# A four-stage language tower on one core: when the stages' semaphores are cleared, and when the experts' scatters may follow each other

## The chip, the core and the metric

The kernel runs on one core of a Trainium2 chip. The metric is the device time of one execution in microseconds. Three runs are known of the kernel before: 2097.66, 2103.85 and 2105.65 us, median 2103.85. The program of a core is five instruction streams: TensorE (PE), VectorE (DVE), ScalarE (ACT), GpSimd (POOL) and SyncE (SP). They meet only at semaphores.

## The reference

Eight sequences of 512 tokens go through a tower of width 192, all in 32-bit floats:

```
h = embedding(x)                                       # 8 x 512 x 192
h = h + rwkv_attention(layernorm(h))
h = h + mixture_attention_ffn(layernorm(h))            # 4 nested experts and 12-head attention
h = h + state_space_block(layernorm(h))
h = h + experts(layernorm(h))

def experts(flat):                                     # 4096 rows of 192
    p, i = top_k(softmax(flat @ Wr), 2); p = p / sum(p)
    for e in 8 experts:                                # the 1280 rows that weigh most
        rows, w = the 1280 best rows of expert e and their weights
        y = (silu(flat[rows] @ w1[e]) * (flat[rows] @ w3[e])) @ w2[e]
        out[rows] += w * y                             # scatter with addition
    return out + (silu(flat @ s1) * (flat @ s3)) @ s2  # the shared expert
```

## The kernel before

The tower is written as four stages, one after the other: `embed_and_route` (embedding, first attention, routing), `moe_attention_ffn`, `state_space_block` and `experts_tower`. Each stage stands in `with kit.phase()` (L42), and inside it has one block with an instruction stream for every engine. At the end of a block all engines drain and meet at a barrier; in the trace its records carry L45. A stage makes its own semaphores through `kit.sem`, which notes them in `kit.used`: 41, 32, 50 and 47 in the four stages. Semaphores that GpSimd's own transfers raise come from `pool_dma_sem`, belong to the whole program and are never cleared. After the stage's block, `phase` opens a second block in which only SyncE has anything to do: it clears the semaphores of `kit.used` one by one (L53). This block too ends with a barrier of all engines (records at L49). Then the next stage begins. SyncE's stream in a stage begins with the loads of weights: L900 in the attention stage, L1602 in the state-space stage, L2384 to L2388 in the experts' stage. Behind them come its waits: for the split parts in `parts_to_scratch` (L906), for the convolution in the state-space stage, for the rows dealt to the experts (`scattered`, L2389) in the last.

The last stage first computes the shared expert for all 4096 rows and routes; GpSimd scatters the rows to a table `dealt` in memory, 1280 slots per expert. The expert loop then takes 40 tiles of 256 rows (`TILES`), five per expert (`CHUNKS`), two blocks of 128 rows each (`CB`). For a tile n:
- SyncE loads the rows (`load_rows`), and TensorE transposes them (`turned_rows`).
- GpSimd takes the rows' weights and numbers out of the tile (`meta`, L2465) into one of two buffers, `w_of` and `row_of`.
- TensorE makes gate and up products (`row_halves`, `whole_rows`), ScalarE the silu (L2943), VectorE the product (`times_gate`).
- TensorE multiplies by w2 (`outputs`, L2877), one tile behind: `outputs(n)` follows `whole_rows(n + 1, 2)`. It waits for VectorE's reading of the tile before (`oe_ready`), as both blocks of a tile lie in one bank of PSUM.
- VectorE weights the two blocks into a buffer `o[:, n % 2]` (`weighted`, L2685).
- GpSimd adds them to the output in memory with two indirect transfers (L2483), one per block, and then waits until both have landed (`stored`, L2488) and raises `oe_free`. So the scatters of two tiles never are in flight together.

`kit.apart` (L59) is a semaphore increment that GpSimd issues ahead of a group of indirect transfers. A wait in the code is taken by the instruction that follows it in the engine's stream.

Of the kernel before, what the change touches and what calls it, by code (L numbers as in the profile page):

```python
# [12 lines left out]
P = 128  # L13
C = 192
# [20 lines left out]
class Kit:  # L35

    def __init__(self, nc, ctx):
        self.nc, self.ctx, self.whole, self.used = nc, ctx, ctx, []

    @contextmanager
    def phase(self):  # L42

        outer, self.used = self.ctx, []
        with ExitStack() as self.ctx:  # L45
            yield self.ctx
        self.ctx = outer

        with self.nc.Block() as block:  # L49
            @block.sync  # L50
            def _(sp):
                for x in self.used:
                    sp.sem_clear(x)  # L53

    def sem(self, name):
        self.used.append(self.ctx.enter_context(self.nc.semaphore(name)))
        return self.used[-1]
# [788 lines left out]
def moe_attention_ffn(kit, a, x1, bands, moe, ssm, spread):  # L846

    nc = kit.nc
    with kit.phase() as ctx:
# [47 lines left out]
        def _(sp):  # L897
            loads = ssm.loads(a)
            for dst, src in loads:
                sp.dma_start(dst, src).then_inc(next_in, 16)  # L900

# [612 lines left out]
def state_space_block(kit, a, ssm):  # L1514

    nc = kit.nc
    with kit.phase() as ctx:
# [80 lines left out]
        @block.sync  # L1598
        def _(sp):
            for dst, src in ((d_skip[:, :], a["d_skip"]), (norm_w[:, :], a["norm_w"]), (w_out[:, :, :], a["w_out"]),  # L1600
                             (wf1[:, :, :], a["wf1"]), (wf2[:, :, :], a["wf2"])):
                sp.dma_start(dst, src).then_inc(loaded, 16)  # L1602
            for t in range(B):
                sp.wait_ge(conv_done, 4 * t + 1)
                if t > 0:
                    sp.wait_ge(w_psum, place["cb", t - 1, 0] + 1)
                    sp.wait_ge(spread_ready, (J - 1) * t)
                sp.dma_start(c_twice[0:DS, :], conv[DS:P, t % 2, 3, :]).then_inc(c_moved, 16)
                sp.dma_start(c_twice[DS:P, :], conv[DS:P, t % 2, 3, :]).then_inc(c_moved, 16)
# [676 lines left out]
def experts_tower(kit, a, dealt, out, out_rows):  # L2286

    nc = kit.nc
    with kit.phase() as ctx:
# [50 lines left out]
        w_of = sb("m_w_of", [P, 2, CB])  # L2340
        row_of = sb("m_row_of", [P, 2, CB], I32)
# [18 lines left out]

        wr_in, s_in, var_ready, rstd_ready, xn_ready, dup_ready, xT_psum, xT_ready, logit_psum = kit.sems(
# [7 lines left out]
        slot_ready, w1_ready = kit.sems("r_slot_ready r_w1_ready")  # L2369
        scattered = kit.pool_dma_sem("s_scattered")  # L2370
        w_in = [kit.sem(f"m_w_in{u}") for u in range(2)]
        x_in = [kit.sem(f"m_x_in{k}") for k in range(2)]
        stored = kit.pool_dma_sem("m_stored")
        meta_ready, xeT_psum, xeT_ready, ge_psum, ge_ready, ue_psum, fe_ready, oe_psum, oe_ready, oe_free = kit.sems(
            "m_meta_ready m_xT_psum m_xT_ready m_g_psum m_g_ready m_u_psum m_f_ready m_o_psum m_o_ready m_o_free")
# [3 lines left out]
        def _(sp):  # L2379
# [7 lines left out]
            for e in range(2):  # L2387
                load_expert(e)  # L2388
            sp.wait_ge(scattered, 2 * NB * 16)  # L2389
# [11 lines left out]
            for n in range(1, TILES):  # L2401
                e, k = n // CHUNKS, n % CHUNKS
                past(sp, xeT_psum, n - 1)
                past(sp, meta_ready, n - 1)
                load_rows(n)
                if k == 1 and 1 <= e < E8 - 1:
                    sp.wait_ge(oe_psum, e * CHUNKS)
                    load_expert(e + 1)

        @block.gpsimd  # L2410
        def _(pool):
# [53 lines left out]
            def meta(n):  # L2465

                pool.wait_ge(x_in[n % 2], (n // 2 + 1) * 32)
                past(pool, oe_ready, n - 1)
                pool.tensor_copy(w_of[:, n % 2, :], xe[:, n % 2, :, 0])
                pool.tensor_scalar(row_of[:, n % 2, :], xe[:, n % 2, :, 1], -1.0, float(N), ALU.mult, ALU.add)\  # L2470
                    .then_inc(meta_ready, 1)

            meta(0)
            for n in range(TILES):
# [5 lines left out]
                pool.wait_ge(oe_ready, n + 1)  # L2480
                kit.apart(pool)
                for r in range(CB):
                    pool.indirect_dma_start(  # L2483
                        out=out_rows, out_offset=bass.IndirectOffsetOnAxis(ap=row_of[:, n % 2, r:r + 1], axis=0),
                        in_=o[:, n % 2, r, :], in_offset=None, bounds_check=N - 1, oob_is_err=False,
                        compute_op=ALU.add).then_inc(stored, 16)

                pool.wait_ge(stored, (n + 1) * CB * 16)  # L2488
                pool.sem_inc(oe_free, 1)

        @block.vector
        def _(dve):
# [209 lines left out]
        def _(pe):  # L2702
# [174 lines left out]
            def outputs(n):  # L2877
# [88 lines left out]
def lm_tower(nc, a, out_rows):  # L2966
# [3 lines left out]
    with ExitStack() as ctx:  # L2970
# [13 lines left out]
        if PHASES > 3:  # L2984
            experts_tower(kit, a, dealt, out, out_rows)
        else:
# [82 lines left out]
```

## Time and profile before

| | |
|---|---|
| profiled execution, its own time | 2098.48 us |
| its span | 2095.7 us |
| mean granted TensorE clock | 0.946 of 2.4 GHz |
| TensorE / VectorE / ScalarE / GpSimd busy | 1893.6 / 1140.6 / 738.5 / 426.4 us |
| stage 1 ends, stage 2 begins | 284.5, 287.1 us |
| stage 2 ends, stage 3 begins | 891.4, 893.9 us |
| stage 3 ends, stage 4 begins | 1326.4, 1329.5 us |
| last matmul ends | 2080.76 us |

The span runs from the first instruction of the execution to the last; the run's own time has 2.8 us more around it. A stage ends where the barrier at L45 releases the engines, and the next one begins where that at L49 does. The expert loop fills the last 500 us.
### The profile page before, as it was taken

The page shows a single profiled execution, that of the slowest core. Times are in us where ns is not written, and L with a number is a line of the kernel's source. Part 1 is how long each engine was busy: PE and PEld are TensorE (multiplying, and loading weights), DVE is VectorE, ACT ScalarE, POOL GpSimd, SP SyncE. Part 2 cuts the span into 40 slices and gives each one's busy share as a digit, 9 for nine tenths or more (in the row PEclk, how much of TensorE's full clock was granted, in tenths as well). Part 3 has the DMA queues.
Part 4 walks back from the last instruction along what each step waited for, and adds up shares of the span by engine and source line. Part 5 has one row for each costly group of instructions (what it writes and reads, how often), then busy time and mean ns, then how long its engine had stood idle before and what let it go on. Part 6 is the DMA issues. An engine that isn't in the chain of part 4 may idle for free. (4 is left out here: it accounts for less than half of the span.)

```text
span 2095.7 us, 28064 instructions
## 1 busy us (share of the span) xinstructions
PE 1893.6 (90%) x10067; PEld 1210.1 (58%) x10075; DVE 1140.6 (54%) x2777; ACT 738.5 (35%) x1248; POOL 426.4 (20%) x567
## 2 busy tenths in 40 slices
PE   4986458999999999879999997799999999999996
PEld 2343432444544444446666665455558888888886
DVE  5898668667666765357888885357222222222221
ACT  1434013554455545445555553131111111211111
POOL 5300210022022101111111111100551223222232
PEclk9988568999999999979999998799999999999998
DMA  3600022111112111000000000200113322222321
GB/s 64 197 31 0 1 64 62 45 54 54 54 39 61 54 54 31 1 32 6 6 11 6 6 6 1 102 1 1 59 53 91 70 58 54 42 63 63 70 38 20
DMA packets 79627, 90.33 MB, mean 43 GB/s; under 512 B 26291, under 2 KB 69493, under 8 KB 78241
## 3 DMA queue, kind: packets, MB, share of 16 engines
q1 hardware_dynamic: 63362, 74.57, 11.5%
q0 software_dynamic: 16128, 13.97, 4.2%
q8 instruction: 80, 1.31, 0.3%
q14 instruction: 57, 0.47, 0.1%
HBM read 54.96 MB, written 34.75 MB: 43 GB/s over the span
## 5 line engine op out<-in xcount | busy, mean ns | idle before, releaser
L1028 DVE TENSOR_REDUCE row_max<-c_ps_m 128x1 f32<-128x512 f32 x384 | 253.2, 687 | 112.1 <-PE c_ps_m L1198 106.7
L1376 ACT ACTIVATE e<-c_ps_s 128x512 f32<-128x512 f32 x384 | 216.4, 596 | 221.1 <-PE c_ps_s L1214 220.4
L2483 POOL DMA_INDIRECT out<-m_o,m_row_of x80 | 125.7, 1571 | 276.2 <-issue 249.6
L2682 DVE TENSOR_TENSOR e_f<-e_ps_u,e_gate 128x512 f32<-128x512 f32 x80 | 55.3, 692 | 205.6 <-PE e_ps_u L2873 205.6
L2883 PE MATMUL e_ps_o<-m_w,e_f 128*128 128x192 f32 x960 | 162.7, 326 | 0.9 <-DVE m_o L2690 0.9
L2943 ACT ACTIVATE e_gate<-e_ps_g 128x512 f32<-128x512 f32 x80 | 47.8, 597 | 325.3 <-PE e_ps_g L2873 325.3
L1198 PE MATMUL c_ps_m<-c_kT,qT 96*128 96x512 bf16 x384 | 150.2, 398 | 10.4 <-DVE row_max L1028 9.5
L1214 PE MATMUL c_ps_s<-qT,c_kT 97*128 97x512 bf16 x384 | 144.6, 386 | 13.0 <-ACT e L1376 5.6
L2883 PEld LDWEIGHTS e_ps_o<-m_w,e_f 128*128 128x128 f32 x960 | 155.1, 190 | 1.2 <-issue 1.2
L2690 DVE TENSOR_SCALAR m_o<-e_ps_o,m_w_of 128x192 f32<-128x192 f32 x80 | 29.7, 413 | 143.5 <-PE e_ps_o L2883 143.5
L1225 PE MATMUL c_ps_a<-e,v 128*32 128x512 f32 x768 | 105.4, 621 | 1.0 <-ACT e L1376 1.0
L1214 PEld LDWEIGHTS c_ps_s<-qT,c_kT 97*128 97x128 bf16 x384 | 36.3, 97 | 106.1 <-ACT e L1376 83.0
L1188 PE MATMUL c_ps_w<-yT,w 96*128 96x512 f32 x192 | 90.5, 596 | 0.5 <-DVE rest L1010 0.5
L2457 POOL DMA_INDIRECT dealt<-e_x,slot x64 | 62.4, 975 | 123.3 <-issue 110.6
L2873 PE MATMUL e_ps_g<-m_xT,m_w 128*128 128x256 f32 x320 | 86.3, 392 | 0.0
L2917 ACT ACTIVATE e_gate<-e_ps_g 128x512 f32<-128x512 f32 x48 | 28.7, 597 | 156.1 <-PE e_ps_g L2729 140.2
L2873 PE MATMUL e_ps_u<-m_xT,m_w 128*128 128x256 f32 x320 | 82.1, 379 | 0.0
L1723 DVE SCALAR_TENSOR_TENSOR conv<-xin,conv_w,conv 128x512 f32<-128x512 f32 x96 | 71.3, 743 | 18.0 <-ACT conv L2140 12.6
L2864 PE MATMUL e_ps_g<-m_xT,m_w 64*128 64x256 f32 x320 | 79.6, 389 | 1.5 <-ACT m_xT L2935 1.5
L2866 PE MATMUL e_ps_u<-m_xT,m_w 64*128 64x256 f32 x320 | 79.6, 389 | 0.0
L2509 DVE TENSOR_TENSOR e_f<-e_ps_u,e_gate 128x512 f32<-128x512 f32 x48 | 33.1, 689 | 79.5 <-ACT e_gate L2917 56.6
L1198 PEld LDWEIGHTS c_ps_m<-c_kT,qT 96*128 96x128 bf16 x384 | 37.7, 98 | 62.2 <-DVE row_max L1028 36.6
(469 smaller groups left out, 4068.1 us busy)
## 6 DMA issues: line engine op xcount, KB each, us to landing
spread<-parts SPq DMA_DIRECT2D x24, 384.0 KB, 2.3
qT<-spread SPq DMA_DIRECT2D x144, 64.0 KB, 2.5
c_kT<-spread SPq DMA_DIRECT2D x144, 64.0 KB, 2.5
m_w<-in_w13e SPq DMA_DIRECT2D x8, 1152.0 KB, 5.1
dealt<-x SPq DMA_DIRECT2D x8, 970.0 KB, 10.6
m_x<-dealt SPq DMA_DIRECT2D x40, 194.0 KB, 2.4
m_w<-in_w2e SPq DMA_DIRECT2D x8, 576.0 KB, 6.2
out<-h SPq DMA_DIRECT2D x8, 384.0 KB, 4.7
```

What stands on the lines that cost most here:

```text
L1028: dve.tensor_reduce(row_max[:, n // J, n % J:n % J + 1], ps_m[:, n % 2, :], AX_X, ALU.max)\
L1188: last = pe.matmul(bank(key), w1[0:CH + c, c, m * P:(m + 1) * P], yT[0:CH + c, c, :], start=c == 0, stop=c == 1)
L1198: pe.matmul(ps_m[:, n % 2, :], qT[0:STACK, h, j * P:(j + 1) * P], kT[0:STACK, h, :], start=True, stop=True).then_inc(m_psum, 1)
L1214: pe.matmul(ps_s[:, n % 2, :], kT[:, h, kc * P:(kc + 1) * P], qT[:, h, :], start=True, stop=True).then_inc(s_psum, 1)
L1225: last = pe.matmul(ps_a[32 * i:32 * i + 32, :], v[:, t % 2, kc, 4 * g + i, :], e[:, (4 * grp + i) % LIVE_E, :], start=kc == 0, stop=kc == ...
L1376: act.activation(e[:, n % LIVE_E, :], ps_s[:, n % 2, :], ACT.Exp, scale=QSCALE).then_inc(e_ready, 1)
L1723: last = dve.scalar_tensor_tensor(out=conv[:, t % 2, m, :], in0=xin[:, m, k:k + T], scalar=conv_w[:, m, k:k + 1], in1=conv[:, t % 2, m, :] ...
L2483: pool.indirect_dma_start(out=out_rows, out_offset=bass.IndirectOffsetOnAxis(ap=row_of[:, n % 2, r:r + 1], axis=0), in_=o[:, n % 2, r, :], ...
L2864: pe.matmul(ps_ge[i][:, k, :], w13e[0:HALF, u, 2, part(m)], xeT[0:HALF, b, 1, :], start=k == 0, stop=False, skip_group_check=True)
L2866: pe.matmul(ps_ue[i][:, k, :], w13e[HALF:P, u, 2, part(m)], xeT[HALF:P, b, 1, :], start=k == 0, stop=False, skip_group_check=True)
L2873: last = pe.matmul(dst[:, k, :], w13e[:, u, w, part(2 * i + k)], xeT[:, b, 0, :], start=False, stop=k == 1, skip_group_check=True)
L2883: last = pe.matmul(ps_oe[:, r, 0:C], fe[:, b, m, r * P:(r + 1) * P], w2e[:, u, m, :], start=m == 0, stop=m == IT - 1)
```

## The change

It has four parts. The clearing of a stage's semaphores is moved: `phase` makes no block of its own any more, and SyncE clears the semaphores of the stage that ended in the next stage, behind the loads with which its stream begins. A stage's semaphores therefore stay taken until the end of the next one. In the last stage, the semaphores of the routing and of the shared expert (33 of them) are cleared by SyncE in the stage itself, behind a wait for the first gate of the last tile, and a block at the very end clears the rest. In the expert loop, GpSimd waits for tile n − 1's landing only after it has issued tile n's scatters, except before the first tile of an expert; for this there are two semaphores `stored`, three buffers for weights and row numbers, and the wait for the weighted rows stands at each scatter, behind `kit.apart`. The last tile's first block of rows goes to another bank of PSUM, and has semaphores of its own, so that it can be weighted and scattered while TensorE makes the second block.

```diff
     def phase(self):
-        outer, self.used = self.ctx, []
+        outer = self.ctx
+        self.used, self.used_ctx = [], ExitStack()
         with ExitStack() as self.ctx:
             yield self.ctx
         self.ctx = outer
-        with self.nc.Block() as block:
-            @block.sync
-            def _(sp):
-                for x in self.used:
-                    sp.sem_clear(x)
+        self.ended_ctx.close()
+        self.ended, self.ended_ctx = self.used, self.used_ctx
+
+    def clear_ended(self, sp):
+        for x in self.ended:
+            sp.sem_clear(x)
...
             for dst, src in loads:                         # and so in the two later stages
                 sp.dma_start(dst, src).then_inc(next_in, 16)
+            kit.clear_ended(sp)
...
-        w_of = sb("m_w_of", [P, 2, CB])
-        row_of = sb("m_row_of", [P, 2, CB], I32)
+        w_of = sb("m_w_of", [P, 3, CB])
+        row_of = sb("m_row_of", [P, 3, CB], I32)
...
+        def rows_out(n, r):
+            return ps_ts[:, 0, 0:C] if n == TILES - 1 and r == 0 else ps_oe[:, r, 0:C]
...
+        routed_first, kit.used = kit.used, []
...
-        stored = kit.pool_dma_sem("m_stored")
+        stored = [kit.pool_dma_sem(f"m_stored{u}") for u in range(2)]
...
+            sp.wait_ge(ge_ready, (TILES - 1) * IP + 1)
+            for x in routed_first:
+                sp.sem_clear(x)
...
             def meta(n):
                 pool.wait_ge(x_in[n % 2], (n // 2 + 1) * 32)
-                past(pool, oe_ready, n - 1)
+                past(pool, oe_ready, n - 2)
...
+            def landed(n):
+                pool.wait_ge(stored[n % 2], (n // 2 + 1) * CB * 16)
...
                 pool.wait_ge(meta_ready, n + 1)
-                pool.wait_ge(oe_ready, n + 1)
+                if n > 0 and n % CHUNKS == 0:
+                    landed(n - 1)
                 kit.apart(pool)
                 for r in range(CB):
+                    if n == TILES - 1 and r == 0:
+                        pool.wait_ge(half_ready, 1)
+                    else:
+                        pool.wait_ge(oe_ready, n + 1)
                     pool.indirect_dma_start(
...
-                        compute_op=ALU.add).then_inc(stored, 16)
-                pool.wait_ge(stored, (n + 1) * CB * 16)
-                pool.sem_inc(oe_free, 1)
+                        compute_op=ALU.add).then_inc(stored[n % 2], 16)
+                if n > 0:
+                    landed(n - 1)
+                    pool.sem_inc(oe_free, 1)
+            landed(TILES - 1)
...
             def weighted(n):
-                dve.wait_ge(oe_psum, n + 1)
                 dve.wait_ge(meta_ready, n + 1)
                 past(dve, oe_free, n - 1)
                 for r in range(CB):
-                    last = dve.tensor_scalar(o[:, n % 2, r, :], ps_oe[:, r, 0:C], w_of[:, n % 2, r:r + 1], None,
+                    halved = n == TILES - 1 and r == 0
+                    if halved:
+                        dve.wait_ge(half_psum, 1)
+                    else:
+                        dve.wait_ge(oe_psum, n + 1)
+                    last = dve.tensor_scalar(o[:, n % 2, r, :], rows_out(n, r), w_of[:, n % 3, r:r + 1], None,
                                              ALU.mult)
+                    if halved:
+                        last.then_inc(half_ready, 1)
                 last.then_inc(oe_ready, 1)
...
-                        last = pe.matmul(ps_oe[:, r, 0:C], fe[:, b, m, r * P:(r + 1) * P], w2e[:, u, m, :],
+                        last = pe.matmul(rows_out(n, r), fe[:, b, m, r * P:(r + 1) * P], w2e[:, u, m, :],
                                          start=m == 0, stop=m == IT - 1)
+                    if n == TILES - 1 and r == 0:
+                        last.then_inc(half_psum, 1)
...
             experts_tower(kit, a, dealt, out, out_rows)
+            with nc.Block() as block:
+                @block.sync
+                def _(sp):
+                    kit.clear_ended(sp)
```

## Rows read from the trace of the kernel before

**Rows 1.** First part of the page: busy us, share of the span, instructions.
```profile
PE 1893.6 (90%) x10067; PEld 1210.1 (58%) x10075; DVE 1140.6 (54%) x2777; ACT 738.5 (35%) x1248; POOL 426.4 (20%) x567
```

**Rows 2.** The clears' line, border by border: count, ns min/median/max, first and last start.
```profile
L53 SPq EVENT_SEMAPHORE_RANGE_CLEAR  x41: 25/29/35, 284.6 to 286.9; - x41
...
L53 SPq EVENT_SEMAPHORE_RANGE_CLEAR  x32: 25/30/49, 891.5 to 893.7; - x32
...
L53 SPq EVENT_SEMAPHORE_RANGE_CLEAR  x50: 25/28/30, 1326.5 to 1329.3; - x50
...
L53 SPq EVENT_SEMAPHORE_RANGE_CLEAR  x47: 25/25/30, 2092.8 to 2095.4; - x47
```

**Rows 3.** The barrier behind the clears, SyncE's release at the three inner borders.
```profile
L49 SPq EVENT_SEMAPHORE  x1: 17/17/17, 287.1 to 287.1; - x1
...
L49 SPq EVENT_SEMAPHORE  x1: 17/17/17, 893.9 to 893.9; - x1
...
L49 SPq EVENT_SEMAPHORE  x1: 17/17/17, 1329.5 to 1329.5; - x1
```

**Rows 4.** A window of the loop: us, PE, PEld, DVE, ACT, POOL busy (instructions), PEclk, DMA, GB/s.
```profile
1900.00:2000.00 100.00, 100.00 (x610) 88.31 (x609) 22.54 (x40) 19.10 (x32) 28.10 (x32) 1.00 0.33 74
```

**Rows 5.** The waits: who waited for whom, us in total, times, longest.
```profile
POOL m_w_of L2469 <- DMA out<-m_o,m_row_of: 83.9, 38, 3.6
```

**Rows 6.** The chain that ended last, from 2076 us: start, us, what.
```profile
2076.60 0.49 issue
...
2077.32 1.58 POOL out L2483
...
2079.20 3.54 DMA out<-m_o,m_row_of
...
2083.71 1.56 POOL out L2483
...
2085.57 1.56 POOL out L2483
```

**Rows 7.** The timeline of the last tile: start, us, engine, line, operation, idle before.
```profile
2076.62 4.14 PE L2883 MATMUL e_ps_o<-m_w,e_f 128*128 128x192 f32 x24 [0.93 <-DVE m_o L2690]
...
2080.79 0.74 DVE L2690 TENSOR_SCALAR m_o<-e_ps_o,m_w_of 128x192 f32<-128x192 f32 x2 [4.32 <-PE e_ps_o L2883]
```

**Rows 8.** GpSimd's drain at the stage ends (L45): the last, then all four.
```profile
L45 POOLq DRAIN  x1: 4137/4137/4137, 2088.4 to 2088.4; - x1
...
L45 POOLq DRAIN  x4: 1109/4677/8352, 242.0 to 2088.4; - x4
```

**Rows 9.** SyncE's timeline in the second stage: last load, first store.
```profile
290.29 0.41 SPq L900 DMA_DIRECT2D neg_a<-in_a_log  x1
...
300.11 2.97 SPq L906 DMA_DIRECT2D spread<-parts  x2
```

**Rows 10.** Windows behind the second inner border, columns as in rows 4.
```profile
890.00:895.00 5.00, 0.97 (x5) 1.00 (x6) 1.92 (x11) 0.21 (x1) 0.00 (x0) 0.66 0.01 2
...
905.00:910.00 5.00, 5.00 (x13) 1.73 (x11) 3.07 (x9) 4.27 (x7) 0.00 (x0) 0.63 0.00 0
...
915.00:920.00 5.00, 1.99 (x13) 1.33 (x15) 4.47 (x11) 1.61 (x3) 0.00 (x0) 0.89 0.01 3
```

**Rows 11.** TensorE's timeline there: the same operations at two times, and a gap.
```profile
894.03 1.94 PE L1905 MATMUL d_ps_w<-ident,d_y 128*128 128x128 f32 x8 [4.92 <-PEq L49]
...
903.15 5.47 PE L1940 MATMUL d_ps_w<-d_yT,w_in 128*128 128x512 f32 x6
...
918.01 0.38 PE L1965 MATMUL d_ps_w<-unpick,d_parts 96*128 96x512 bf16 x1 [3.17 <-DVE d_parts L1715]
...
927.79 1.06 PE L1905 MATMUL d_ps_w<-ident,d_y 128*128 128x128 f32 x8
...
943.75 2.82 PE L1940 MATMUL d_ps_w<-d_yT,w_in 128*128 128x512 f32 x6
```

More of the change, by code:

```diff
@@ L38, in __init__ @@
     def __init__(self, nc, ctx):
-        self.nc, self.ctx, self.whole, self.used = nc, ctx, ctx, []
+        self.nc, self.ctx, self.whole = nc, ctx, ctx
+        self.used, self.used_ctx = [], ctx
+        self.ended, self.ended_ctx = [], ExitStack()
     @contextmanager
     def phase(self):
-        outer, self.used = self.ctx, []
+        outer = self.ctx
+        self.used, self.used_ctx = [], ExitStack()
         with ExitStack() as self.ctx:
@@ L47, in phase @@
         self.ctx = outer
-        with self.nc.Block() as block:
-            @block.sync
-            def _(sp):
-                for x in self.used:
-                    sp.sem_clear(x)
+        self.ended_ctx.close()
[3 more added lines that the diff above has]
+            sp.sem_clear(x)
     def sem(self, name):
-        self.used.append(self.ctx.enter_context(self.nc.semaphore(name)))
+        self.used.append(self.used_ctx.enter_context(self.nc.semaphore(name)))
         return self.used[-1]
@@ L2372, in experts_tower @@
         x_in = [kit.sem(f"m_x_in{k}") for k in range(2)]
-        stored = kit.pool_dma_sem("m_stored")
-        meta_ready, xeT_psum, xeT_ready, ge_psum, ge_ready, ue_psum, fe_ready, oe_psum, oe_ready, oe_free = kit.sems(
-            "m_meta_ready m_xT_psum m_xT_ready m_g_psum m_g_ready m_u_psum m_f_ready m_o_psum m_o_ready m_o_free")
+        stored = [kit.pool_dma_sem(f"m_stored{u}") for u in range(2)]
+        meta_ready, xeT_psum, xeT_ready, ge_psum, ge_ready, ue_psum, fe_ready, oe_psum, oe_ready, oe_free, half_psum, half_ready = kit.sems(
+            "m_meta_ready m_xT_psum m_xT_ready m_g_psum m_g_ready m_u_psum m_f_ready m_o_psum m_o_ready m_o_free m_half_psum m_half_ready")
         block = ctx.enter_context(nc.Block())
@@ L2388, in _ @@
                 load_expert(e)
+            kit.clear_ended(sp)
             sp.wait_ge(scattered, 2 * NB * 16)
@@ L2467, in meta @@
                 pool.wait_ge(x_in[n % 2], (n // 2 + 1) * 32)
-                past(pool, oe_ready, n - 1)
-                pool.tensor_copy(w_of[:, n % 2, :], xe[:, n % 2, :, 0])
-                pool.tensor_scalar(row_of[:, n % 2, :], xe[:, n % 2, :, 1], -1.0, float(N), ALU.mult, ALU.add)\
+                past(pool, oe_ready, n - 2)
+                pool.tensor_copy(w_of[:, n % 3, :], xe[:, n % 2, :, 0])
+                pool.tensor_scalar(row_of[:, n % 3, :], xe[:, n % 2, :, 1], -1.0, float(N), ALU.mult, ALU.add)\
                     .then_inc(meta_ready, 1)
+            def landed(n):
+                pool.wait_ge(stored[n % 2], (n // 2 + 1) * CB * 16)
             meta(0)
@@ L2479, in _ @@
                 pool.wait_ge(meta_ready, n + 1)
-                pool.wait_ge(oe_ready, n + 1)
+                if n > 0 and n % CHUNKS == 0:
+                    landed(n - 1)
                 kit.apart(pool)
                 for r in range(CB):
+                    if n == TILES - 1 and r == 0:
+                        pool.wait_ge(half_ready, 1)
+                    else:
+                        pool.wait_ge(oe_ready, n + 1)
                     pool.indirect_dma_start(
-                        out=out_rows, out_offset=bass.IndirectOffsetOnAxis(ap=row_of[:, n % 2, r:r + 1], axis=0),
+                        out=out_rows, out_offset=bass.IndirectOffsetOnAxis(ap=row_of[:, n % 3, r:r + 1], axis=0),
                         in_=o[:, n % 2, r, :], in_offset=None, bounds_check=N - 1, oob_is_err=False,
-                        compute_op=ALU.add).then_inc(stored, 16)
-                pool.wait_ge(stored, (n + 1) * CB * 16)
-                pool.sem_inc(oe_free, 1)
+                        compute_op=ALU.add).then_inc(stored[n % 2], 16)
[3 more added lines that the diff above has]
+            landed(TILES - 1)
         @block.vector
@@ L2985, in lm_tower @@
             experts_tower(kit, a, dealt, out, out_rows)
+            with nc.Block() as block:
+                @block.sync
+                def _(sp):
+                    kit.clear_ended(sp)
         else:
```

## Prediction

> **What bounds the kernel now.** The page's first part shows TensorE busy for 90% of the span [rows 1], but an average over four stages says little about edits that sit at stage borders and in the last tile. So I read the borders next: the records of the three helper lines that make one. L45 is the end of a stage's block (all engines meet there), L53 the clears, L49 the end of the block that only clears. At the three inner borders SyncE makes 41, 32 and 50 clears, the first at 284.6, 891.5 and 1326.5 us, and the block around them lets the engines go at 287.1, 893.9 and 1329.5 us [rows 2, 3]. Between those times no engine does anything: this is path by construction, since each engine waits at both ends.
>
> Then the expert loop, where most of the diff sits. In 1900 to 2000 us TensorE is busy 100.00 of 100.00 us [rows 4]; GpSimd waits 38 times for a scatter to land, 83.9 us in all [rows 5], but TensorE waits for none of it. Only the last tiles count. The chain of waits for the end [rows 6] reads: scatter of tile 38, two issues from 2077.32 and 2079.20; the second one's landing, at 2079.20 + 3.54 = 2082.74; then tile 39's two issues, the last ending at 2085.57 + 1.56 = 2087.13. TensorE had finished tile 39 at 2076.62 + 4.14 = 2080.76 and VectorE had weighted it by 2081.53 [rows 7]. So from 2077 us GpSimd's own queue sets the end. Behind it stands a border once more: GpSimd's drain from 2088.4, 4.14 us long, then 47 clears from 2092.8 to 2095.4 us [rows 2, 8].
>
> **The change part by part.**
> *Three inner borders.* The block of clears goes. The next stage starts where the first clear starts now: 287.1 − 284.6 = 2.5, 893.9 − 891.5 = 2.4 and 1329.5 − 1326.5 = 3.0 us, together 7.9 us. From below: the barrier at L45 stays, and is not in these numbers. From above: nothing more can go, since that barrier stands right behind the old stage's last work. The first work after a border depends only on the barrier, not on a transfer issued earlier, so it moves with it.
>
> *The clears in their new place.* SyncE makes them behind the loads of the next stage: 41 × 2.3/40 = 2.4 us in the attention stage. What is queued behind them on SyncE is the first store of the split parts, L906. The loads end at 290.29 + 0.41 = 290.7; L906 starts at 300.11 [rows 9] and waits for VectorE, so 9.4 us lie free and 2.4 are used. In the other two stages SyncE's next step comes later still and the clears are 32 and 50. Cost nothing; without that cover it would be the length of the clears, 2.2 to 2.8 us per stage, once. The 33 clears of the routing semaphores (9 + 7 + 7 + 8 + 2 names) wait for the gate of the last tile's first pair and take 33 × 0.057 = 1.9 us, while GpSimd still has two tiles to scatter: nothing.
>
> *The last border.* 47 − 33 = 14, plus the two new names half_psum and half_ready, leaves 16 clears behind the last tile. One clear costs 2.6/46 = 0.057 us [rows 2], so 31 fewer give 1.8 us.
>
> *No wait for the landing between two tiles of one expert.* In the loop this frees GpSimd and nothing else. At the end it takes 2082.74 − 2080.76 = 2.0 us out of the chain [rows 6]. What is late next: GpSimd itself. Its four scatters of 1.56 to 1.58 us with 0.30 between the two of a tile and 0.97 (2083.71 − 2082.74) between tiles then follow each other. At the expert borders the wait for the tile before stays in front of the scatter, but that scatter was issued a tile (12.5 us, four GpSimd instructions per tile and 32 in 100 us [rows 4]) earlier, longer than any landing wait here (3.6 at most [rows 5]).
>
> *Where the wait stands.* Now the wait for the weighted tile is taken at the semaphore increment (L62), and 0.49 us pass behind it before the scatter's register move [rows 6]. In the new order the increment comes first and the wait sits right at the scatter, so that this 0.49 could pass before the data are there: 0 to 0.5 us at tile 38; I take 0.4. Against it, each scatter of a pair now has a wait of its own. The gap of 0.30 may stay, or grow to 0.30 + 0.49 at each of two pairs: 0 to 1.0 us lost. I take 0.1, as the gap of 0.30 already holds the same register move and comes from the scatter alone.
>
> *Last tile in two halves.* TensorE's start on tile 39 still waits for VectorE's reading of tile 38 [rows 7]. Half of its 4.14 us is done by 2078.7, the weighting of that half by 2079.2; but GpSimd is only free for it at about 2076.9 + 1.58 + 0.30 + 1.56 + 0.97 = 2081.3. The whole tile is weighted at 2081.5 as it is. So the halves are worth 0.2 to 0.6 us at most; that is inside the chain as I wrote it, and adds nothing.
>
> *Landing and drain.* The last landing now takes 2088.4 − 2087.13 = 1.3 us at most; tile 38's took 2.0. With two tiles in flight it may be the longer one: 0 to 0.7 lost, I take 0.2. The drain of GpSimd is 1.1 to 8.4 us at the four borders (median 4.7) [rows 8], and I have no row that says what sets it: −3.0 to +4.2 us. I keep it at 4.1, since what stands before it is unchanged.
>
> *Other extra buffers* (three for weights and row numbers, the third bank for half a tile) cost no instruction. VectorE gets one more wait per tile in a stretch where it is a fifth busy.
>
> Sum: 7.9 + 1.8 + 2.0 + 0.4 − 0.1 − 0.2 = 11.8 us. The profiled execution took 2098.48 us with a span of 2095.7, so one like it would take 2086.7 with a span of 2083.9. It lies 5.4 below the median of the three runs (2097.66, 2103.85, 2105.65); against the median the sum gives 2103.85 − 11.8 = 2092.0. The runs of one kernel spread by 8 us, so a few us either way in the median say nothing of the sum.
>
> **The rivals.**
> *The clock stays up across the second inner border.* The granted clock falls there: 0.66 on average in 890 to 895 us, with TensorE idle from about 889 to 894, and comes back within 905 to 910 [rows 10, 11]. The same transposes take 1.94 us there and 1.06 later, the same six input products 5.47 and 2.82 [rows 11]: 0.9 + 2.65 = 3.5 us, and with the products between them about 5. The change shortens the idle time from 4.9 to 2.5 us, and it may be too short for the fall. For: the shortest idle gap that I found ahead of a fall is 3.2 us (before 918.01, the mean of 915 to 920 us is 0.89) [rows 10, 11]. Against: the work behind the border is thin, eight transposes and then small products. At the other two borders TensorE stands still longer, before the change and after it. Time: 2092 − 5 = 2087. The Trainium skill (TensorE: Matmul & The Clock Gate, Part 1) says that the low clock is the default and activity lifts it; by that rule the shorter gap can only help, and the trace does not decide at this length.
>
> *The clears were a cover for something.* While SyncE clears, the other engines stand at the next barrier with their queues filled. If a new stage's first instructions are not there in time, each border gives back what it won, up to its 2.4 to 3.0 us; with two thirds of the 7.9 gone the time is 2092 + 5.3 = 2097, with all of it 2100. For it: only that the trace cannot show a stage that starts behind one barrier after much work. Against: engines that left their last work long ago have had time, and after L49 the first instruction starts within 0.2 us (893.9, then 894.03) [rows 3, 11]. The Trainium skill (Runtime: NRT & Kernel Launch, Instruction fetch mechanics) says that instructions are prefetched in sequence and a taken branch out of the window stalls for a fetch. By that rule a border with its branch could stall at the new place; the short gap behind L49 neither shows nor excludes it.
>
> *The overlap gives the wait back at the end.* The last landing waits for more transfers (0.7), each pair's gap is the long one (1.0), and the drain takes what GpSimd no longer waited for (2.0): 11.8 − 3.7 = 8, time 2096.
>
> *Slower than before.* The mechanism would be the clock: every stage runs earlier, and the falls, which now come after idle gaps, come at other places. One fall costs half its length where TensorE is the bound (the 17 us after the second border: about 5 us). To lose 11.8 and more, three such falls must be new; it decides from there. Price: one new fall 2097, four 2092 + 20 = 2112. Against it: in the expert loop TensorE runs without gaps [rows 4], and no fall can start there. That the drain doubles to its longest (8.4) alone gives 2096.
>
> **How the numbers follow.** Forecast 0.46 (2092, own range 2087 to 2096), clock stays up 0.20 (2087), cover lost in part or whole 0.20 (2097 to 2100), overlap given back 0.10 (2096), slower 0.04. A measurement of this kernel can tell 0.5% (10.5 us) from no change: under 2093.3 is faster. That holds for six tenths of the forecast and nearly all of the clock case, with a little from the others: 0.30 + 0.19 + 0.06 = 0.55. Slower by over 0.5% (above 2114) 0.03, the rest, 0.42, within. The range 2082 to 2100 leaves out 1 in 10 on each side.
>
> **What would show it.** In the profile after: one barrier per inner border, with clears between loads on SyncE while others work, and the next stage's first instruction within 0.2 us of the release at L45; stages shifted by 2.5, 4.9 and 7.9 us; the last four scatters back to back with no landing between; 16 clears behind the drain; span 2084. Wrong it would be if the first instruction of a stage came over 1 us after the barrier, if GpSimd's drain left 4 us by more than one, if the last scatter ended more than 8.5 us behind TensorE's start on tile 39 (10.5 now), or if TensorE's clock in 892 to 905 were 1.00.

## The result, and the profile after

The kernel after takes 2090.78 us (median of 5 runs, 2088.3 to 2093.26), the kernel before on the same chip 2101.13 (5 runs). The ratio is 0.9945, 95% interval 0.9926 to 0.9964: 11.6 us by the ratio (7.6 to 15.5), 10.35 between the medians. Forecast were 2092.0 us and a gain of 11.8, counted from the 2103.85 that was then the median of three runs.

The profiled execution took 2090.77 us, its span is 2089.1, the mean clock 0.947. First the page's busy times, to be held against [rows 1]:

```profile
PE 1900.4 (91%) x10067; PEld 1214.0 (58%) x10075; DVE 1140.5 (55%) x2777; ACT 739.3 (35%) x1248; POOL 427.9 (20%) x567
```

The instructions are the same in number. TensorE is busy 6.8 us longer in this execution, 5.6 of it in stage 1, where its mean clock was 0.81 and before 0.83. The borders, after, in the view of the groups (count, ns, first and last start; L48 is now the barrier at a stage's end, L57 `clear_ended`, L2422 the 33 routing clears, L3018 the end of the last block; an EVENT_SEMAPHORE of SPq is SyncE's release at a barrier). They answer to [rows 2, 3, 8]:

```profile
L48 SPq EVENT_SEMAPHORE  x1: 17/17/17, 287.5 to 287.5; - x1
...
L57 SPq EVENT_SEMAPHORE_RANGE_CLEAR  x41: 25/30/44, 290.9 to 293.2; - x41
...
L48 SPq EVENT_SEMAPHORE  x1: 17/17/17, 891.6 to 891.6; - x1
...
L48 SPq EVENT_SEMAPHORE  x1: 17/17/17, 1326.5 to 1326.5; - x1
...
L2422 SPq EVENT_SEMAPHORE_RANGE_CLEAR  x33: 25/30/39, 2065.7 to 2067.9; - x33
...
L48 POOLq DRAIN  x1: 4227/4227/4227, 2083.5 to 2083.5; - x1
...
L48 SPq EVENT_SEMAPHORE  x1: 17/17/17, 2087.8 to 2087.8; - x1
...
L57 SPq EVENT_SEMAPHORE_RANGE_CLEAR  x16: 25/28/30, 2087.9 to 2088.8; - x16
...
L3018 SPq EVENT_SEMAPHORE  x1: 17/17/17, 2089.0 to 2089.0; - x1
```

There is one release per inner border. The stages do not begin 2.5, 4.9 and 7.9 us earlier, as the prediction's signs have it: they begin at 287.5, 891.6 and 1326.5, which is 0.4 later, 2.3 earlier and 3.0 earlier, and the span is 2089.1, not 2084. The end of this section takes that up. The timeline of the kernel after (start, us, engine, line, operation, idle before) shows what follows it, and then the last two tiles; it answers to [rows 7, 9, 11]:

```profile
287.60 0.36 SPq L904 DMA_DIRECT2D lnw<-in_ln  x1
...
300.50 0.33 SPq L911 DMA_DIRECT2D spread<-parts  x1
...
891.74 1.94 PE L1911 MATMUL d_ps_w<-ident,d_y 128*128 128x128 f32 x8 [2.43 <-PEq L48]
...
911.60 0.40 PE L1956 MATMUL d_ps_w<-log_a,d_ones 128*128 128x24 f32 x2 [0.25 <-DVE log_a L1702]
...
933.85 2.19 PE L2023 MATMUL d_ps_w<-dtx_rest,b_tm 128*64 128x192 f32 x12 [7.27 <-DVE w_out L1886]
...
1326.60 0.34 SPq L2394 DMA_DIRECT2D wr<-in_wr  x1
...
2074.29 2.19 PE L2913 MATMUL e_ps_ts<-m_w,e_f 128*128 128x192 f32 x12 [1.03 <-DVE m_o L2718]
...
2074.92 1.58 POOL L2505 DMA_INDIRECT out<-m_o,m_row_of  x1 [8.16 <-DVE m_o L2718]
...
2076.31 2.11 PE L2913 MATMUL e_ps_o<-m_w,e_f 128*128 128x192 f32 x12
...
2076.61 0.42 DVE L2718 TENSOR_SCALAR m_o<-e_ps_ts,m_w_of 128x192 f32<-128x192 f32 x1 [2.47 <-PE e_ps_ts L2913]
...
2076.81 1.56 POOL L2505 DMA_INDIRECT out<-m_o,m_row_of  x1 [0.31 <-issue]
...
2078.47 0.42 DVE L2718 TENSOR_SCALAR m_o<-e_ps_o,m_w_of 128x192 f32<-128x192 f32 x1 [1.43 <-PE e_ps_o L2913]
...
2078.67 1.56 POOL L2505 DMA_INDIRECT out<-m_o,m_row_of  x1 [0.30 <-issue]
...
2080.54 1.56 POOL L2505 DMA_INDIRECT out<-m_o,m_row_of  x1 [0.30 <-DMA out<-m_o,m_row_of]
```

A stage's first instruction starts 0.1 us behind the release (287.5 to 287.60, 891.6 to 891.74, 1326.5 to 1326.60). At the end four scatters run back to back, 0.30 us apart. TensorE's start on tile 39 to the end of the span is 2095.7 − 2076.62 = 19.1 us before and 2089.1 − 2074.29 = 14.8 after.

The two spans differ by 6.6 us only. Worked out: the three gaps between old and new release, 2.6 + 2.5 + 3.1 = 8.2, and 4.3 at the end make 12.5. Against this, stage 1 is 287.5 us long and was 284.5, stage 3 is 434.9 and was 432.5, the expert stage up to tile 39 is 0.7 longer, stage 2 is 0.2 shorter. Whether the change did that, or whether executions differ by as much, is the first question.

### The profile page after: what moved, and what is told of

The parts are those of the page before. It is cut to its first block and busy times, and to the rows that moved or that the text cites. A ratio compares the mean times of both kernels' runs of the same rounds, so it can differ in the third digit from the quotient of the medians.

```text
span 2089.1 us, 28031 instructions
## 1 busy us (share of the span) xinstructions
PE 1900.4 (91%) x10067; PEld 1214.0 (58%) x10075; DVE 1140.5 (55%) x2777; ACT 739.3 (35%) x1248; POOL 427.9 (20%) x567
## 5 line engine op out<-in xcount | busy, mean ns | idle before, releaser
L1203 PE MATMUL c_ps_m<-c_kT,qT 96*128 96x512 bf16 x384 | 150.6, 399 | 10.5 <-DVE row_max L1033 9.4
L1729 DVE SCALAR_TENSOR_TENSOR conv<-xin,conv_w,conv 128x512 f32<-128x512 f32 x96 | 71.3, 743 | 19.0 <-ACT conv L2146 13.6
```

The source lines that it names most:

```text
L1203: pe.matmul(ps_m[:, n % 2, :], qT[0:STACK, h, j * P:(j + 1) * P], kT[0:STACK, h, :], start=True, stop=True).then_inc(m_psum, 1)
L1729: last = dve.scalar_tensor_tensor(out=conv[:, t % 2, m, :], in0=xin[:, m, k:k + T], scalar=conv_w[:, m, k:k + 1], in1=conv[:, t % 2, m, :] ...
```

## The experiments

Every ratio is against the kernel before, run on the same chip in the same round; the rounds used several chips, so kernels of different rounds are compared by their ratios and by their traces. The edits are shown in part, the longer ones cut at `...`, and against the kernel after, or against x5_better where the heading says so.

**x4_after_again: is the longer stage 1 and 3 the change's doing?** No edit.

> The changed kernel once more, unedited, for a second profile and more times. Theory A (the first stage's 287.5 us against 284.5 and the state-space stage's 434.9 against 432.5 are scatter from run to run): these two lengths come out different by a us or more from the first profile of the changed kernel, while the second stage stays at 604. Theory B (the change made them longer): 287 to 288 and 434 to 436 us again. Median 10 to 12 us under the kernel before.

Ratio 0.9944 (0.9932 to 0.9957), 2092.03 us. Its profiled execution was the slowest of the five. Stage 1 took 290.0 us in it, and 284.5 to 290.0 over all kernels here, whose stage 1 holds the same work: 284.5 in before and in x11_drain20, 285.0 in x7_drain, 287.2 in x2_overlap, which has the old borders. The clock goes with it: the mean over stage 1 is 0.83 in before and in x11_drain20, 0.81 in the kernel after and in x2_overlap, 0.80 here. So the 3.0 us of stage 1 are scatter between executions. Stage 3 took 435.3 us here, close to the first profile's 434.9, which theory A did not expect (nor the 605.7 of stage 2). What speaks for scatter there is x2_overlap: its borders are the old ones, and its stage 3 took 436.0. All profiles but that of before lie at 434.4 to 436.1. So before's 432.5 was most likely a quick execution; with two profiles of the old borders that is likely, not shown.

**x1_borders: the three inner borders alone.** The loop and the last tile are as before, and all clears of the last stage stand at its end.

```diff
-        routed_first, kit.used = kit.used, []
...
-        stored = [kit.pool_dma_sem(f"m_stored{u}") for u in range(2)]
+        stored = kit.pool_dma_sem("m_stored")
...
-                if n > 0:
-                    landed(n - 1)
-                    pool.sem_inc(oe_free, 1)
-            landed(TILES - 1)
+                pool.wait_ge(stored, (n + 1) * CB * 16)
+                pool.sem_inc(oe_free, 1)
```

> The kernel before with the borders of the change alone: clears inside the next stage, all 47 of the last stage behind it, the expert loop as before. Theory A (the sum by places): the three inner borders give 2.5 + 2.4 + 3.0 = 7.9 us and nothing else moves, so the median is 7.9 us under the kernel before, stages 2 and 4 keep their lengths (604 and 763 us between the barriers) and the 47 clears behind the last barrier still take 2.6 us. Theory B (the second border gives part back through the clock: in the profile of the changed kernel the state-space stage is 434.9 us long against 432.5): 5.5 us. Theory C (a cover is lost at each border): under 4 us, and the first instructions of a stage over 0.5 us behind its barrier.

2095.11 us, ratio 0.9963 (0.9951 to 0.9976): 7.8 us (5.0 to 10.3), where 7.9 were forecast. By the time alone theory B (5.5) is not excluded; that the borders themselves give the whole is read from the releases. This profile is also the one in which the clock stayed up longest behind the second border. Its windows (us, busy of PE, PEld, DVE, ACT, POOL, PEclk, DMA share, GB/s):

```profile
890.00:895.00 5.00, 2.44 (x18) 2.24 (x20) 4.27 (x19) 3.08 (x4) 0.99 (x1) 0.92 0.34 87
895.00:900.00 5.00, 5.00 (x18) 2.26 (x17) 3.55 (x10) 2.59 (x2) 3.88 (x6) 0.73 0.49 192
900.00:905.00 5.00, 4.70 (x13) 1.29 (x11) 3.16 (x9) 3.65 (x6) 0.00 (x0) 1.00 0.00 0
```

and its timeline there:

```profile
891.46 1.06 PE L1911 MATMUL d_ps_w<-ident,d_y 128*128 128x128 f32 x8 [2.43 <-PEq L48]
...
910.09 0.40 PE L1956 MATMUL d_ps_w<-log_a,d_ones 128*128 128x24 f32 x2 [1.43 <-DVE log_a L1702]
...
932.34 2.19 PE L2023 MATMUL d_ps_w<-dtx_rest,b_tm 128*64 128x192 f32 x12 [7.28 <-DVE w_out L1886]
```

The transposes take 1.06 us against 1.94 in the kernel after, whose same windows show 0.65, as low as before's 0.66 [rows 10], and then 0.50:

```profile
890.00:895.00 5.00, 2.39 (x11) 2.02 (x11) 4.24 (x20) 2.27 (x4) 0.71 (x1) 0.65 0.30 68
895.00:900.00 5.00, 5.00 (x17) 2.98 (x18) 3.56 (x9) 3.52 (x2) 4.17 (x6) 0.50 0.53 211
900.00:905.00 5.00, 5.00 (x10) 2.69 (x11) 2.18 (x8) 1.83 (x4) 0.00 (x0) 0.50 0.00 0
```

The idle gap is 2.43 us in both. In windows of half a us the clock of x1_borders falls only at 894.2, with TensorE at work again, and is back at 897.7: 3.4 us at 1.2 GHz. In the kernel after it is down from 891.5, while TensorE still stands idle, to 905.1: 13.6 us. What the 10 us more of full clock bought: from the transposes to the L2023 group TensorE is busy 27.0 us against 29.6, but gets there in 40.9 us against 42.1, since ahead of L1956 it now waits 1.43 us for VectorE instead of 0.25. Of 2.5 us less work, 1.2 us remain. From L1956 on both run in step, and the stage is 434.4 us long against 434.9. So the clock was worth 0.5 to 1.2 us, not 5.

**x6_clears_first: does the clears' place on SyncE cost anything?** At the start of each stage they stand ahead of the loads, not behind.

```diff
+            kit.clear_ended(sp)
             for dst, src in loads:
                 sp.dma_start(dst, src).then_inc(next_in, 16)
-            kit.clear_ended(sp)
```

> The changed kernel with SyncE's clears ahead of the next stage's loads instead of behind them, so that the loads are issued 1.8 to 2.9 us later. Theory A (neither the loads nor the clears are on the path): stage lengths as in the changed kernel (604, 435, 748 us up to TensorE's start on the last tile, each within 1.5 us), median the same within 0.1%. Theory B (the first loads of a stage are nearly due): one stage longer by up to the 1.8 to 2.9 us of its clears, so a median 2 to 7 us higher.

2089.35 us, ratio 0.9932 (0.9914 to 0.9949), releases at 287.3, 891.4, 1326.3 and 2088.0 us. Stages 2 and 3 are 604.1 and 434.9 us long, exactly as in the kernel after, and the last 761.7 against 761.3. Even with 2.3 us of clears in front, the loads are in time. The place costs nothing, in either order.

**x8_routed_late: what are the 33 early clears worth?**

```diff
-            for x in routed_first:
-                sp.sem_clear(x)
+            kit.used[:0] = routed_first
```

> The changed kernel with the 33 semaphores of routing and shared expert cleared at the very end with the 16 others. Sum: 49 clears instead of 16 behind the last barrier, 33 x 0.057 = 1.9 us more there, the rest unchanged. Rival: the clears inside the stage were not free before (they stood ahead of SyncE's arrival at the barrier), then under 1.9 us.

One time, 2093.14 us; the reading is from the trace. From the last stage's release to that of the last block it is 3.1 us (2087.1 to 2090.2), in the kernel after 1.2. The 33 early clears are worth 1.9 us.

**x2_overlap: the overlap of the scatters alone,** with the old borders and no halves.

```diff
-        self.ended_ctx.close()
-        self.ended, self.ended_ctx = self.used, self.used_ctx
+        with self.nc.Block() as block:
+            @block.sync
+            def _(sp):
+                for x in self.used:
+                    sp.sem_clear(x)
...
-            return ps_ts[:, 0, 0:C] if n == TILES - 1 and r == 0 else ps_oe[:, r, 0:C]
+            return ps_oe[:, r, 0:C]
```

> The kernel before with the overlap of two tiles' scatters alone: borders as before, the last tile not halved. From TensorE's start on the last tile to the end of the last scatter it was 10.5 us before and is 7.8 in the changed kernel. Theory A (the landing wait of 2.0 us and most of the gap of 0.97 go, and the halves matter little): 8.5 us or less, so 2 us or more gained over the whole. Theory B (without halves the scatter of the last tile waits for its weights, ready 4.7 us behind TensorE's start and picked up 0.7 later): its first scatter starts 5.3 us behind TensorE's start and the last ends at 8.8, so 1.7 us gained. Theory C (overlap costs at the landing or the drain): the drain of GpSimd over 5 us long.

2102.34 us (12 runs), ratio 0.9995 (0.9986 to 1.0005): 1.1 us, not clear of nothing by the times. The trace has the end of it:

```profile
2084.46 4.14 PE L2902 MATMUL e_ps_o<-m_w,e_f 128*128 128x192 f32 x24 [1.03 <-DVE m_o L2707]
...
2092.13 1.56 POOL L2494 DMA_INDIRECT out<-m_o,m_row_of  x1 [0.30 <-issue]
```

TensorE's start on tile 39 to the last scatter's end is 2093.69 − 2084.46 = 9.2 us, before 10.5; theory A had 8.5 or less, theory B 8.8. So the overlap is worth 1.3 us at the end, and the drain behind it, 4.2 us, is not longer than theory C's 5. The stage up to tile 39 is 748.5 us long, not shorter than before's 747.1, so nothing is won in the loop. The 2.0 + 0.4 − 0.1 of the sum were too much.

**x3_no_halves: the whole change without the last tile's halves.**

```diff
-            return ps_ts[:, 0, 0:C] if n == TILES - 1 and r == 0 else ps_oe[:, r, 0:C]
+            return ps_oe[:, r, 0:C]
...
-                    if n == TILES - 1 and r == 0:
-                        last.then_inc(half_psum, 1)
```

> The changed kernel without the halves of the last tile. Theory A (halves worth 0.2 to 0.6 us, as forecast): the last tile's first scatter starts 0.2 to 0.6 us later behind TensorE's start than the 4.38 us of the changed kernel. Theory B (the 0.5 us of issue behind a wait is paid again, since the queue of GpSimd stands at the wait): 1.0 us later, at 5.4. Median within 1 us of the changed kernel either way.

2089.69 us, ratio 0.9941 (0.9928 to 0.9954): by the medians nothing is lost. The timeline of its last tile does show a loss:

```profile
2073.31 4.14 PE L2913 MATMUL e_ps_o<-m_w,e_f 128*128 128x192 f32 x24 [1.03 <-DVE m_o L2718]
...
2077.59 0.74 DVE L2718 TENSOR_SCALAR m_o<-e_ps_o,m_w_of 128x192 f32<-128x192 f32 x2 [4.43 <-PE e_ps_o L2913]
...
2079.11 1.56 POOL L2505 DMA_INDIRECT out<-m_o,m_row_of  x1 [1.72 <-DVE m_o L2718]
...
2080.97 1.56 POOL L2505 DMA_INDIRECT out<-m_o,m_row_of  x1 [0.31 <-issue]
```

GpSimd stands idle for 1.72 us ahead of the last tile: it is free at 2077.39, 4.1 us behind TensorE's start, and waits for the weighted rows. With halves its first scatter starts 4.38 us behind TensorE's start, without them 5.80. That is 1.4 us, more than either theory had (0.2 to 0.6, or 1.0), and as much at the end (7.81 against 9.22); it is too little for the medians to show.

**x7_drain: what is in GpSimd's last drain?** Two fills are put between the last landing and the drain; their length is read from the trace.

```diff
             landed(TILES - 1)
+            for i in range(2):
+                pool.memset(x1[:, 8 * i:8 * i + 8, :], 0.0)
```

> The changed kernel with two fills of 128 x 2064 elements on GpSimd behind the landing of the last scatter, ahead of the stage's drain (a few us of work; the drain took 4.2 us there). Theory A (the drain waits for what the last scatter leaves to do in GpSimd, whatever comes behind it): the barrier releases 5.7 us after the last scatter's end as now, and the drain is shorter. Theory B (the drain costs 4.2 us in itself behind indirect transfers): the release is later by the length of the fills. Theory C (the fills queue behind what is left, so both add up): the fills themselves end 4 us or more after they could start.

```profile
2080.89 3.57 POOL L2515 MEMSET e_x<- 128x2064 f32 x2 [1.22 <-DMA out<-m_o,m_row_of]
```

```profile
L48 POOLq DRAIN  x1: 7821/7821/7821, 2080.9 to 2080.9; - x1
```

One time, 2092.91 us; the reading is from the trace. The drain's record starts with the fills, so its length includes what was queued. It ends 4.25 us behind them (2088.71 against 2084.46), which is theory B. The 4.2 us are therefore not the transfers' landing, which lies before the fills; they are the drain's own. In stage 2 and 3 of before, where GpSimd makes no indirect transfer, it ends 0.1 us behind the last operation (863.64 and 863.7; 1304.94 and 1305.04), in stage 1, with 32 gathers, 2.6 us behind. That suggested a cost per indirect transfer, and with it an experiment: drain earlier, where GpSimd has slack.

**x10_after_drain38: the kernel after with one more drain, at tile 38.**

```diff
             for n in range(TILES):
+                if n in (TILES - 2,):
+                    pool.drain()
```

> The changed kernel with one edit: an explicit drain of GpSimd at the start of tile 38. Theory A (a drain works off what the indirect transfers since the last drain left): the one at tile 38 takes 4 us or more behind the last scatter, within the 8.6 us that GpSimd has there, the one at the stage's end 0.4 instead of 4.2 us, and the median is 3.9 us under the changed kernel, 14 to 15 us under the kernel before. Theory B (in x9_drain_early the drain at tile 20 was needed too): the last drain stays above 2 us. Theory C (140 transfers take longer than GpSimd's slack, at the 0.07 us each that 104 took: 10 us): the scatter of tile 38 starts late, and 1 to 2 us of the gain are lost.

2085.53 us, ratio 0.9923 (0.991 to 0.9937), where the kernel after has 0.9945 and 0.9944. The intervals still touch, so the size is read from the trace:

```profile
L2493 POOLq DRAIN  x1: 8280/8280/8280, 2063.4 to 2063.4; - x1
...
L48 POOLq DRAIN  x1: 383/383/383, 2083.7 to 2083.7; - x1
```

The last drain falls from 4.23 to 0.38 us. The early one ends 5.2 us behind the end of the last scatter issue ahead of it, in slack: tile 38's first scatter still waits 2.79 us for its weighted rows. Theory C's 10 us for 140 transfers did not come.

**x5_better: the other two waits at the end.** The halves for the last two tiles, and the 16 clears made by SyncE in the stage itself once both `stored` are there, while GpSimd drains. The final block is gone (its removal, and the waits of GpSimd and VectorE for the new halves, are not shown).

```diff
-            return ps_ts[:, 0, 0:C] if n == TILES - 1 and r == 0 else ps_oe[:, r, 0:C]
+            return ps_ts[:, 0, 0:C] if n >= TILES - 2 and r == 0 else ps_oe[:, r, 0:C]
...
+            for u in range(2):
+                sp.wait_ge(stored[u], TILES // 2 * CB * 16)
+            sp.wait_ge(oe_free, TILES - 1)
+            for x in kit.used:
+                sp.sem_clear(x)
...
-                past(pe, oe_ready, n)
+                if n < TILES - 1:
+                    past(pe, oe_ready, n)
+                else:
+                    pe.wait_ge(half_ready, 1)
```

> The changed kernel with two more steps: the first block of the last two tiles (not of the last alone) goes to the other bank and is weighted and scattered by itself, and TensorE's start on the last tile waits only for the reading of that block, not for the whole of tile 38; and SyncE clears the 16 remaining semaphores behind the landing of the last scatters, so the block at the very end is gone. Theory A (GpSimd's chain of four scatters starts too late because the first waits for a whole tile, and GpSimd's drain of 4.2 us covers the clears): the last scatter ends 11.0 us behind TensorE's start on tile 38 instead of 12.9, and the 1.2 us behind the last stage's barrier go: 3.1 us under the changed kernel. Theory B (the drain waits for something that does not begin earlier, so the earlier scatters are given back there): only 1.2 us. Theory C (the clears meet the drain and lengthen it): the drain over 5 us.

2086.52 us, ratio 0.9919 (0.9901 to 0.9937). The last scatter's issue ends 10.8 us behind TensorE's start on tile 38, in the kernel after 12.9, as theory A has it. The clears lie at 2081.0 to 2081.9 beside the drain (2081.2 to 2085.4), and the span ends with the barrier at 2085.6.

**x9_drain_early: x5_better with drains at tiles 20 and 38.**

```diff
+                if n in (20, TILES - 2):
+                    pool.drain()
```

> The kernel x5_better with two explicit drains of GpSimd in the expert loop, at the start of tile 20 and of tile 38, where GpSimd waits 8.6 us for the next weights anyway. The drain at the stage's end takes 4.2 us behind GpSimd's last work, with or without fills ahead of it; the drains that ended the two middle stages, which have no indirect transfers, took 0.1 us behind the last work, that of the first stage 2.6. Theory A (a drain cleans up what all indirect transfers since the last one left, by their number): the drain at tile 38 is short, the one at the end, behind four scatters, is short too, and the median falls by up to 4 us under x5_better. Theory B (a drain behind any indirect transfer costs 4.2 us, however few there were): all three take 4.2 us, the end stays, and the median is that of x5_better within 0.1%. Theory C (the drain in the loop pushes GpSimd past its slack): the last scatter ends later than 10.8 us behind TensorE's start on tile 38.

2082.39 us, ratio 0.9892 (0.9876 to 0.9909). This beats both kernels: 1.1% under before, and by the two ratios 0.5% under after. Against x5_better the intervals touch; the traces show its last drain fall from 4.23 to 0.37 us.

```profile
L2498 POOLq DRAIN  x1: 10563/10563/10563, 1837.4 to 1837.4; - x1
...
L2498 POOLq DRAIN  x1: 6533/6533/6533, 2063.2 to 2063.2; - x1
...
L48 POOLq DRAIN  x1: 373/373/373, 2081.3 to 2081.3; - x1
```

The drain at tile 20 ends 7.5 us behind the last scatter's issue, the one at tile 38 3.5 us, neither of them short as theory A had it for tile 38; both lie in slack.

**x11_drain20: x5_better with the drain at tile 20 alone.**

```diff
+                if n in (20,):
+                    pool.drain()
```

> The kernel x5_better with the explicit drain at the start of tile 20 alone; 40 indirect transfers follow it. Measured so far: 32 transfers, drain 2.6 us behind the last work; 36, 3.5; 104, 7.5; 4, 0.4; but 144 at the end of the stage, 4.2. Theory A (0.07 to 0.1 us per transfer since the last drain, some of it worked off on the way once many have gathered): the last drain takes 2.9 to 3.9 us, a little under the 4.2 of x5_better. Theory B (a part of the cost is paid once, and the drain at tile 20 pays it): under 1 us.

The last drain now has 40 transfers behind the one at tile 20, and takes 3.3 us, as theory A has it:

```profile
L48 POOLq DRAIN  x1: 3323/3323/3323, 2078.7 to 2078.7; - x1
```

One time, 2083.93 us, says no more than that it is not slower than x5_better.

## Why the prediction was right

The place held, and so did the size: 11.8 us forecast, 11.6 measured by the ratio. That it comes this close is partly luck: two errors in the last tiles cancel, and the time of 2092.0 was counted from a median of 2103.85 that five runs put at 2101.13. Step by step:

- *Inner borders, 7.9 us.* x1_borders alone gives 7.8 (5.0 to 10.3), the releases 8.2. Right, and for the reason given: the time lay between two barriers at which every engine waited.
- *Clears in their new place, nothing.* Right. In the attention stage they end at 293.2, and SyncE's next step comes at 300.50. x6_clears_first shows more slack than was claimed: the loads themselves can wait, too.
- *31 fewer clears, 1.8 us.* Right. The 33 of x8_routed_late cost 1.9, and behind the last stage's release 3.0 us have become 1.2.
- *No landing between tiles 38 and 39, 2.0; wait at the scatter, 0.4; gaps, −0.1.* Together 2.3 forecast, 1.3 measured (x2_overlap). The larger error is in the 2.0: it ran from the landing back to the end of TensorE's work (2080.76), but a scatter needs the weighted rows, and those are there at 2081.53 [rows 7]. So 2082.74 − 2081.53 = 1.2 us were to be had. The smaller one is the wait's place. The pick-up, the time from the met wait to the scatter's start, is not done ahead of the wait: tile 38's scatter starts 0.85 us behind the end of its weighting before and 0.78 after, so the 0.4 was 0.1 at most. The chain of waits of the kernel after still has it in front ("issue" is time in which GpSimd waits for nothing that the profile shows):

```profile
2074.21 0.51 issue
2074.71 0.03 POOLq L2505
2074.74 0.18 issue
2074.92 0.34 POOL out L2505
```

- *Halves, nothing in the sum.* They are worth 1.4. The step that failed was that GpSimd "is only free for it at about" 2081.3: it put the 0.97 us between two tiles, which is the pick-up behind a landing. With no landing to wait for the gap is 0.30, GpSimd is free before the whole tile is weighted, and the data are late instead. The two errors, −1.0 and +1.4, nearly cancel, which is luck: 2.7 us measured for scatters and halves together, where 2.3 stood.
- *Landing and drain, −0.2.* From the last scatter's end to the drain 1.4 us, to be held against 1.3, and 4.23 against 4.14: right. But "I have no row that says what sets it" was too quick. The drain's three other lengths in [rows 8] are mostly work that was queued; had I looked for GpSimd's last operation at each border, 0.1, 0.1 and 2.6 us would have been left. That points to the indirect transfers, whose number the change leaves as it is, and so to a range narrower than −3.0 to +4.2.
- *The clock stays up (chance 0.20, 2087 us).* It fell in all eleven profiles with the short gap, in x1_borders 2.8 us and in x7_drain 1.3 us behind the first transpose. Its price was wrong, too. I added up slower TensorE operations of [rows 11], but TensorE also waits for VectorE in that stretch, ahead of L1956, and half of the 2.5 us that the slower operations lose is slack there: 10 us more of full clock gave x1_borders 1.2 us at most. The Trainium skill (TensorE: Matmul & The Clock Gate, Part 1) has the low clock as the default that activity lifts. The granted clock of 0.65 in 890 to 895 us behind a gap of 2.43 us does not speak against that, and no run here isolates it. The shorter gap was not enough here: 13.6 us at the low clock in the kernel after.
- *The clears were a cover (0.20).* Refuted: the first instruction starts 0.1 us behind the release at each of the three borders, and x1_borders gives the whole 7.8. The Trainium skill (Runtime: NRT & Kernel Launch, Instruction fetch mechanics) tells of a stall at a branch out of the prefetched window; at these borders no such stall is seen.
- *Overlap given back (0.10) and slower (0.04).* Neither came. The last transfers landed 0.1 us later at most, and the pairs' gaps stayed at 0.30. Stage 1 has a lower clock in the profile after (0.81 against 0.83), but so has x2_overlap with the old borders, and x11_drain20 with the new ones has 0.83.

In the sum: 8.2 at the borders (release to release), 2.7 at the scatters, 1.7 to 1.9 at the clears, −0.1 each for landing and drain make 12.4 to 12.6, the 12.5 found above; the ratio says 11.6.

## What to carry to other kernels

Work between two barriers at which every engine waits is path, however small; bookkeeping that only one engine does belongs beside the next stage's work. Before a slower instruction is priced, look who is waited for next: part of what a low clock loses ahead of a wait for another engine is slack, here at least half of 2.5 us. Before a drain is taken as fixed, subtract the work queued under its record; what is left may be moved into slack by draining earlier.

## What the runs showed of the hardware

GpSimd's drain has a cost of its own behind indirect transfers, which up to some forty of them grows with their number since the last drain. Where all of them had landed, its end lies behind the last landing or operation by 0.1 us with none, 0.37 with 4, 2.6 with 32, 3.3 with 40 and 4.1 to 4.2 with 144. The drains in the loop come while the last two transfers may still be landing, so they are measured from the end of the last issue: 3.5 us with 36, 7.5 with 104 and 5.2 with 140; on that count the 144 at the end take 5.4 to 5.6. Up to 104 that is 0.07 to 0.1 us for each; why 140 and 144 take less than 104 is open. The 32 are gathers, and 64 of the 104, 140 and 144 are scatters to `dealt`, so number and kind are not told apart. That an early drain takes this from the end is shown (x10_after_drain38, x9_drain_early); what GpSimd does in it is not.

Each clear takes SyncE 0.057 us (46 intervals in 2.6 us [rows 2]), and a barrier of all engines lets the next stage begin 0.1 us behind its release. A gap of 2.43 us in TensorE's work, with the same program text on both sides, was followed by a fall to the lower clock in all eleven profiles that have it, but not at the same moment: at 891.5, still inside the gap, in the kernel after, 2.8 us behind it in x1_borders. The low stretch was 13.6 us long in the one and 3.4 in the other.
